# Two transformer stages in one block: the end of an expert stage and the first turns of attention

## The reference, cut to what matters

```
x = x + retention(layernorm(x))             # 8 heads, chunks of 64
x = x + experts(layernorm(x))               # 16 experts of width 256, top 1, and a shared expert
x = x + attention(layernorm(x))             # 16 heads of 8, with biases, softmax over 256 keys
x = x + routed_block(layernorm(x), ...)     # 31 picked tokens of a sequence pass a small transformer

def attention(h):
    q, k, v = h @ Wq.T + bq, h @ Wk.T + bk, h @ Wv.T + bv
    probs = softmax(einsum('bqhd,bkhd->bhqk', q * SCALE, k))
    return einsum('bhqk,bkhd->bqhd', probs, v).reshape(b, s, d) @ Wo.T + bo
```

## Time and profile before

| | |
|---|---|
| median of three runs | 1081.19 us (1079.97 to 1082.27) |
| profiled execution | 1078.87 us, of which its span 1077.1 us |
| mean granted TensorE clock | 0.946 |
| instructions | 29674 |
| end of the experts' last matmul, first instruction of attention | about 440.2, 452.4 us from the span's start |
| first score matmul of attention, end of the last | 478.15, about 956 us |
| first instruction of the routed phase | 975.25 us |

### The profile page before, as it was taken

One profiled execution on the slowest core, in us unless ns is written; L12 is line 12 of the kernel. 1 busy time (PEld: TensorE's weight loads), 2 busy tenths in 40 slices (PEclk: granted clock), 3 DMA queues, 4 the chain that ended last, 5 costly groups with the idle time before them and its releaser, 6 DMA issues. The chain is left out here.

```text
span 1077.1 us, 29674 instructions
## 1 busy us (share of the span) xinstructions
PE 966.2 (90%) x9858; PEld 719.6 (67%) x9858; DVE 706.7 (66%) x1509; ACT 640.8 (59%) x1320; POOL 707.9 (66%) x1531
## 2 busy tenths in 40 slices
PE   6999999689989999359999999999999999963776
PEld 5888888479956776235777777767777767632554
DVE  5878787675534444226788787788787788835752
ACT  4676666422223444125788888888888888752552
POOL 4667676367735555457688888888888888534003
PEclk9999999799999999757999999999999999996898
DMA  8600000131123332263444444444444445302000
GB/s 317 258 3 2 3 2 2 61 90 53 52 74 83 82 83 67 72 197 112 115 124 140 125 133 121 129 125 139 126 130 123 126 127 140 99 19 59 12 3 21
DMA packets 84165, 100.91 MB, mean 94 GB/s; under 512 B 10590, under 2 KB 68158, under 8 KB 83646
## 3 DMA queue, kind: packets, MB, share of 16 engines
q1 hardware_dynamic: 78782, 87.97, 27.5%
q0 software_dynamic: 5248, 11.15, 3.2%
HBM read 61.78 MB, written 36.47 MB: 91 GB/s over the span
## 5 line engine op out<-in xcount | busy, mean ns | idle before, releaser
L1322 DVE TENSOR_REDUCE a_neg_max<-a_slot 128x4 f32<-128x1024 f32 x256 | 306.7, 1220 | 112.6 <-PE a_slot L1464 86.7
L1409 ACT ACTIVATE a_pT<-a_slot 128x1024 f32<-128x1024 f32 x256 | 255.3, 1024 | 13.5 <-PE a_slot L1480 6.6
L1464 PE MATMUL a_slot<-a_k_stack,a_q_stack 72*128 72x256 bf16 x1024 | 159.1, 280 | 4.5 <-DMA a_k_stack<-part_dram 3.9
L1480 PE MATMUL a_slot<-a_q_stack,a_k_stack 75*128 75x256 bf16 x1024 | 151.1, 275 | 2.2 <-DVE a_neg_max L1322 0.9
L1495 PE MATMUL a_ps_o<-a_pT,a_v_pad 128*32 128x256 f32 x2048 | 141.6, 386 | 0.0
L1464 PEld LDWEIGHTS a_slot<-a_k_stack,a_q_stack 72*128 72x128 bf16 x1024 | 96.3, 100 | 49.1 <-issue 25.5
L703 POOL DMA_INDIRECT y_rows<-m_total,m_token x80 | 76.5, 957 | 66.2 <-ACT m_total L856 52.3
L1480 PEld LDWEIGHTS a_slot<-a_q_stack,a_k_stack 75*128 75x128 bf16 x1024 | 93.2, 98 | 35.5 <-ACT a_pT L1409 14.2
L326 DVE TENSOR_TENSOR r_score<-ps_score,r_decay 128x512 f32<-128x512 f32 x128 | 81.5, 679 | 7.7 <-PE ps_score L478 7.6
L1495 PEld LDWEIGHTS a_ps_o<-a_pT,a_v_pad 128*32 128x32 f32 x2048 | 64.7, 109 | 27.5 <-issue 13.0
L696 POOL DMA_INDIRECT sorted_in<-h,m_slot x64 | 63.9, 998 | 26.1 <-issue 18.6
(11 more groups left out here) (292 smaller groups left out, 2127.0 us busy)
## 6 DMA issues: line engine op xcount, KB each, us to landing
a_q_stack<-part_dram SPq DMA_DIRECT2D x64, 288.0 KB
a_k_stack<-part_dram SPq DMA_DIRECT2D x64, 288.0 KB
part_dram<-a_part SPq DMA_DIRECT2D x64, 192.0 KB, 2.7
sorted_in<-h SPq DMA_DIRECT2D x10, 528.0 KB, 13.2
m_xe<-sorted_in SPq DMA_DIRECT2D x40, 132.0 KB, 2.2
expert_up<-in_eu_dram SPq DMA_DIRECT2D x1, 4096.0 KB, 24.9
part_dram<-a_part SPq DMA_DIRECT2D x64, 64.0 KB, 3.7
out_dram<-e_x_plus_h SPq DMA_DIRECT2D x32, 128.0 KB, 2.5
```

The source lines that it names most:

```text
L1322: nc.vector.tensor_reduce(neg_max[:, p, half, t, g * UNIT:(g + 1) * UNIT], slots[SLOT_OF["m", j]][:], AX.X, ALU.max, negate=True).then_inc ...
L1409: nc.scalar.activation(pT[:, j % PT_RING], slots[SLOT_OF["e", j]][:], ACT.Exp).then_inc(e_read, 1)
L1464: ins = nc.tensor.matmul(slots[SLOT_OF["m", j]][:, q], q_stack[0:QK_ROWS, p, half, head, t * P:(t + 1) * P], k_stack[0:QK_ROWS, p, half, h ...
L1480: ins = nc.tensor.matmul(slots[SLOT_OF["e", j]][:, q], k_stack[0:EXP_ROWS, p, half, head, t * P:(t + 1) * P], q_stack[0:EXP_ROWS, p, half, ...
```

## The change

mixture_phase and attention_phase now write into one `Block` and keep their semaphores to the end of it, in a `Memory` called `both`. There is no drain, no clearing and no barrier between them; the buffers of the experts and of `early` are given back, and those of attention lie on the same addresses as before. In the place of the barrier each of POOL, DVE, ACT and PE begins attention with a wait for y_loaded[0], the first load of expert outputs, which SP issues only when all scatters have been stored.

Expert outputs are loaded in ten groups (2, 2, 4 and seven times 8 tiles) and not in six (2, 2, 4, 8, 16, 32). Four are issued at the start, the other six one by one at SP's turns 4, 8, ... 24, as the last step of the turn. SP writes the rows of ones at turn 4, between fill(1) of sequence 0 and store_parts of sequence 1, and no longer ahead of turn 0. For sequences 0 and 1 the moments come in their own turn (lag 0) and POOL's inv_std one turn sooner (lag 1), ahead of the splits. The memsets of v_pad go from DVE's turns 0 and 1 to its turns 2 and 3.

```diff
 class Memory:
-    def __init__(self, nc):
+    def __init__(self, nc, holder=None):
...
     def __exit__(self, *e):
         self.ctx.__exit__(*e)
+        if self.holder is not None:
+            self.holder.sems += self.sems
+            return
         self.nc.clear_and_free_semaphores(self.sems)
         self.nc.all_engine_barrier()
...
-LOAD_SIZES = (2, 2, 4, 8, 16, 32)
+LOAD_SIZES = (2, 2, 4) + (8,) * 7
+FIRST_LOADS = 4
...
         @block.sync
         def _(sp):
-            for n in range(EARLY_LOADS, len(Y_LOADS)):
+            for n in range(EARLY_LOADS, FIRST_LOADS):
                 load_y(sp, keep, n)
-            sp.wait_ge(preset, 4)
-            for p in range(2):
-                for half in range(HALVES):
-                    sp.dma_start(k_stack[QK_ROWS:EXP_ROWS, p, half], ones_b[:]...).then_inc(ones_in, 16)
+            def load_later(s, p, r):
+                n = s // 4 + FIRST_LOADS - 1
+                if s % 4 == 0 and FIRST_LOADS <= n < len(Y_LOADS):
+                    load_y(sp, keep, n)
+            def fill_ones(s, p, r):
+                if s == 0:
...
+                    (the wait and the four DMAs above)
...
-            pipeline(sp, [(fill(1), 4), (store_parts, 3), (store_out, 9), (give_max(1), 5),
-                          (fill(0), 3), (give_max(0), 4)], B, B)
+            pipeline(sp, [(fill(1), 4), (fill_ones, 4), (store_parts, 3), (store_out, 9), (give_max(1), 5),
+                          (fill(0), 3), (give_max(0), 4), (load_later, 0)], B, B)
...
         @block.gpsimd                      # and so at the head of vector, scalar and tensor
         def _(pool):
+            pool.wait_ge(y_loaded[0], 16)
...
-            pipeline(pool, [(split_max(0), 5), (weigh, 9), (add_given, 0), (split_qk(0), 3), (inv_std, 2),
+            pipeline(pool, [(split_max(0), 5), (weigh, 9), (add_given, 0), (inv_std_early, 1), (split_qk(0), 3), (inv_std, 2),
                             (split_max(1), 5), (split_qk(1), 3), (bias, 5), (pad_v, 4), (inv_std3, 8)], B, B)
...
-                           (settle3, 7), (maximum(6), 4), (settle, 0), (maximum(7), 4), (preset_v_pad, 0)], B, B)
+                           (settle3, 7), (maximum(6), 4), (settle, 0), (moments_early, 0), (maximum(7), 4),
+                           (preset_v_pad, 2)], B, B)
...
         retention_phase(nc, w, keep)
-            mixture_phase(nc, w, keep)
-        attention_phase(nc, w, keep, out)
+        with Memory(nc) as both:
+            block = both.ctx.enter_context(nc.Block())
+            mixture_phase(nc, w, keep, block, both)
+            early.holder = both
+            early.__exit__(None, None, None)
+            attention_phase(nc, w, keep, out, block, both)
```

## The result

The changed kernel takes 1077.90 us (median of 6 runs, 1076.95 to 1078.27); the kernel before took 1081.24 in the 6 runs beside it (1079.97 to 1082.27). The ratio is 0.997 (0.996 to 0.9981): 3.3 us faster, where 7.7 had been forecast. So the two spans (1076.3 and 1077.1) differ by only 0.8, and sums are compared here from mark to mark, not by the spans.

The account below looks back on a forecast made before the run. TensorE, busy 90% of the span, was taken to bound the kernel outside the gaps between stages. Savings of 4.3, 2.1 and 1.35 us sum to 7.75, rounded to 7.7: from 1081.19 to 1073.5 us, range 1069 to 1077.5.

Parts of the forecast that it names:

- Left alone: Full turns stay as they are; attention's exit, clearing some 40 more semaphores, costs 0, with 1.9 us as bound.
- Term 1: End of the experts' stage: engines wait for y_loaded[0], not drain and barrier; attention starts 4.3 us sooner.
- Term 2: First layer norm of attention: ACT starts it 3.6 us after attention's start, not 5.73; 2.1 us less.
- Term 3: POOL's order: sequence 1's inverse deviation no longer stands between sequence 0's k and q splits; 1.35 us less.
- The ones: Rows of ones on SP's queue: four issues of 0.74 us, using slack only; fill(0) of sequence 1 still 6.9 sooner.
- The later loads: Six 512 KB loads on SP, one every fourth turn, hidden in slack: 0 us, bound 20.
- rival C: Later loads push fill(1) past its slack on SP and its DMA ring, six times: 1102 us; chance 0.05.
- Rival A: TensorE's clock in attention's ramp rises sooner (to 1066.5 us, chance 0.11) or later (1076.5, chance 0.12).
- Rival B: First norm's or POOL order's saving at attention's start is lost to a hidden hand-off: 1077 us; chance 0.14.
- three signs of being wrong: Full turns over 14.7 us at a load, clock rise not 22 us from first scores, fill(0) of sequence 1 waited for.

Follow-up runs that it names:

- run 2: The kernel before, without the GpSimd drain at the end of the experts' block, barriers and clearing kept: 1075.41 us, ratio 0.9961.
- run 14: The changed kernel with its two blocks kept apart and without the GpSimd drain of the experts' block: 1074.34 us, ratio 0.9945.
- run 1: The changed kernel without the GpSimd drain at the end of the joined block: 1073.04 us, ratio 0.9939.
- run 10: The changed kernel with the joining taken back (two blocks, drain, clearing and barriers between), its other parts kept: 1102.9 us, ratio 0.9974, on another chip.
- run 3: The kernel before with 41 more unused semaphores allocated in attention and cleared at its exit: 1081.32 us, ratio 1.0004.
- run 6: The kernel before with one unused indirect gather issued by POOL in attention's block: 1107.63 us on another chip, ratio 1.0006.
- run 8: The changed kernel without the GpSimd drains of the joined block and the routed phase: 1098.36 us, ratio 0.9916; taken again 1099.27, ratio 0.9941; on other chips.
- run 4: The changed kernel with all ten loads of expert outputs issued at the start of attention: 1078.10 us, ratio 0.9981.
- run 11: The changed kernel without both GpSimd drains, plus twelve useless matmuls ahead of the first scores: 1099.75 us, ratio 0.9943 against 0.9941 without them.

## Why the prediction was wrong

The direction was right and the size was not. 7.7 had been forecast and 3.3 came; the time, 1077.90, lies just outside the range, which ended at 1077.5.

**The step that failed is "Left alone".** It took the exit of attention at 0, with a bound of 1.9 from the cleared semaphores; it grew by 4.53. The step priced what the block clears and never asked what its end waits for. Term 1 had named "drain, clearing of semaphores, barrier, and a second barrier" as the content of the 6.49 and let all of it go. But the joined block still ends with a drain, and still has the 144 indirect stores in it. Two lines of the page, the same before and after, had their count:

```profile
y_rows<-m_total,m_token POOLq DMA_INDIRECT x80, 2.2
sorted_in<-h,m_slot POOLq DMA_INDIRECT x64
```

The comparison was there as well: the earlier trace rows is an exit with none of them on POOL (2.79), attention's exit another (3.43), and the experts' gap, even counted from SP's load (the landing of the last store had set that off), was 6.49. The rows can't split that gap; runs 2 and 14 did: 3.96 are the drain, and what else ends a block takes 0.4 beyond the 2.1 of the load's landing.

**Term 1 as a saving in the gap** came as forecast: 4.39 for 4.3. It was a true reading of the wrong quantity, since the same wait was still to come.

**Term 2** said start + 3.6: +3.62 (runs 1, 10, 14: +3.60, +3.59, +3.58). POOL was through with its additions at start + 1.91 (forecast 1.9) and DVE with the first moments at start + 2.06 (forecast 2.1).

**Term 3** said 1.35. The eight split steps of sequence 0 follow on each other, 457.88 to 463.57, and what stood between k and q is gone: 1.34. The three terms measured 4.39, 2.11 and 1.34, together 7.84, and SP issued the first fill just that much sooner (19.39 after its first load, before 27.23). The first scores came only 7.41 sooner, since this fill took 5.43 from its first issue to them and 5.00 before. Other profiles of the old code have 5.12 to 5.49 there (runs 2, 3 and 6), others of the new one 5.48 to 6.14 (runs 1 and 8); whether the change has a part in it stays open.

**The ones** were to take 0.74 each, so that fill(0) of sequence 1 would come 6.9 sooner: four took 3.06, and the fill was issued 29.95 after SP's first load, before 36.83: 6.88. TensorE did wait for it, but 0.18 us, and in this execution alone; the profiles of runs 1 and 8 have no such wait:

```profile
482.43 1.03 PE L1492 MATMUL a_slot<-a_k_stack,a_q_stack 72*128 72x256 bf16 x4 [0.18 <-DMA a_k_stack<-part_dram]
```

**The later loads** were to cost nothing. One of them in SP's queue and the turn around it, in the changed kernel, against the earlier trace rows:

```profile
600.54 0.78 SPq L1177 DMA_DIRECT2D a_q_stack<-a_max_T  x1
601.36 0.43 SPq L575 DMA_DIRECT2D h<-y_rows  x1
603.06 0.80 SPq L1165 DMA_DIRECT2D a_q_stack<-part_dram  x1
```
```profile
596.63 0.61 PE L1492 MATMUL a_slot<-a_k_stack,a_q_stack 72*128 72x256 bf16 x4
...
611.35 0.61 PE L1492 MATMUL a_slot<-a_k_stack,a_q_stack 72*128 72x256 bf16 x4
```

The issue took 0.43, not 1.36 (that one stood behind 4 MB), within the gap of 1.74; the turn is 14.72. One turn, the second with a load in it, was 14.97 for 14.65. That isn't rival C at work: runs 1 and 8 issue the same load in the same turn, and from the fill behind it to the same fill a turn later they have 14.63 in all three profiles, where the changed kernel has 14.90. The Trainium skill (DMA: Bandwidth & Descriptors, "Queues, rings and completion order") has an engine take its descriptors in ring order, which spoke for C; no row here shows that order, and run 4 finds no price.

**Rival A** (the clock). In the changed kernel the clock rose 7 us after the first scores, fell back and rose again, in the same columns:

```profile
478.00:479.00 1.00, 0.87 (x5) 0.47 (x4) 1.00 (x2) 0.64 (x2) 0.77 (x4) 0.79 0.09 25
482.00:483.00 1.00, 0.82 (x5) 0.43 (x4) 0.64 (x1) 0.00 (x0) 0.92 (x3) 0.50 0.37 107
495.00:496.00 1.00, 1.00 (x8) 0.65 (x7) 0.27 (x3) 0.40 (x2) 0.00 (x0) 0.76 0.51 201
```

So the distance of 22 us from the first scores was no constant (final rise at 495.5, 24 after them; in run 1 at 492.4, 20.5 after them; in run 4 at 494.5, 23 after them). An early rise that falls back brought nothing that run 11 could measure: DVE paces the first turns. The text of A had given DVE's 15 busy of 22 us as the limit and up to 7 us to gain; in run 11's first 8 us at full clock DVE was at 7.22. The final rise is another matter. In the four profiles with this attention code it came 48.6, 46.2, 46.0 and 45.3 us after SP's load (changed kernel, run 8 twice, run 1), and attention's work ended at +519.68, 517.96, 517.75 and 517.16, in the same order. A later rise went with a longer attention; no run here moved that rise on purpose, so that it is the cause isn't shown. **Rival B** had the right total (1077) for a wrong reason: nothing of terms 2 and 3 was lost. What was missing among the rivals is that the change does not remove its wait but moves it. The prediction's three signs of being wrong all came up in some measure (one turn of 14.97 with a load in it, the distance of the clock's rise, the wait for fill(0) of sequence 1), but none of them made the miss; the exit of attention, which did, was not among them.

## What to carry to other kernels

When two stages are joined to be rid of what stands between them, list what the end of a block waits for, and look where each item goes. Here the drain of GpSimd was paid at the end of the block that held POOL's DMAs, however early these had landed, and it moved with that end; left out there, it was not paid at the next one. Price the new exit as carefully as the old gap. If a block's POOL DMAs are all awaited by semaphores anyway, leaving its drain out was worth more here (4.0 us in the gap, ratio 0.9961, one argument of one line) than the whole joining (nothing by the marks, ratio 0.9987). And compare stretches from mark to mark and totals by the medians only; if a second profile of the same code exists, look at it before a difference of a us or two is given a cause.

## What the runs showed of the hardware

The drain of GpSimd has a price after POOL's indirect DMAs have long landed, and among gathers of one size it grows with their number: exits of 3.43 us with none in the block, 3.48 with 1, 3.77 with 32, 8.98 with 96 gathers or 96 scatters of 1 KB rows (12.6 MB), 7.96 with the experts' 144 stores of rows of about half a KB (9.6 MB). The last two groups have 4608 packets each. Without the drain the exits of blocks that held the 144 stores are 3.46 (run 1) and, in the gap, 2.53 from SP's load (run 2), and no later exit is longer for it (3.13, 3.14). The exit also waits some 2.5 us for the last output store, behind which a short drain hides, so the law can't be read from these five points. By bytes the three exits of 3.77 (4.2 MB), 7.96 and 8.98 would fit some 0.64 to 0.73 us per MB, an estimate from these exits less 0.9 for the rest of an exit (3.43 less 2.5); number of DMAs alone doesn't fit (96 cost more than 144). What the drain does in that time no row shows, and no run varied the bytes at a fixed number.

TensorE's clock in the ramp of the changed kernel rose, fell and rose again within 17 us: TensorE was busy 1.00 of each us from 472 to 478 ahead of the first rise, 0.53 to 0.87 of each from 478 to 482 ahead of the fall, and 1.00 of each from 488 on ahead of the last rise at 495.5. After the first stage's exit, at the same code, it rose anywhere from 213.4 to 216.4. The Trainium skill (TensorE: Matmul & The Clock Gate, "The HAM clock gate") has sustained matmuls release the throttle; the fillers of run 11 did (0.99 from 492.5 to 500.5, behind 3.97 us of wide matmuls), while the scores of the kernel before, 20.68 busy of 22 us, did not for 22 us. What tells the two apart isn't settled here.
